# Convolved attention of a decoder on one NeuronCore: mixes of two pairs of tiles taken together, a third buffer for the turned probabilities, one buffer for the taps

## The chip, the cores and the metric

The kernel runs on one core of a Trainium2 chip. The metric is the device time of one execution in microseconds, the median of several; smaller is better. The core has TensorE (PE, with weight loads listed apart as PEld), VectorE (DVE), ScalarE (ACT), GpSimd (POOL) and SyncE (SP), which here only issues DMA. The engines run their own instruction streams in order and wait for each other through semaphores.

## The reference

A decoder of two layers on x (4 x 1024 x 256) with six stages: causal attention, attention to a context, a quantized feed-forward, the convolved attention that the change touches, attention with latents, and a feed-forward with eight experts. The touched stage, with 16 heads of 16 features:

```
def _L1_attn_ref(query, Wq, bq, Wk, bk, Wv, bv, Wo, bo, conv_w, conv_b):   # H=16, DH=16, KS=3
    Q, K, V = heads of query @ W.T + b
    scores = jnp.einsum('bhqd,bhkd->bhqk', Q, K) / np.sqrt(dh)
    x = scores.transpose(0, 2, 1, 3).reshape(b * s, h, s)
    x = lax.conv_general_dilated(x, conv_w, window_strides=(1,), padding=[(1, 1)],
                                 dimension_numbers=('NCW', 'OIW', 'NCW'))
    x = x + conv_b[None, :, None]
    weights = jax.nn.softmax(x.reshape(b, s, h, s).transpose(0, 2, 1, 3), axis=-1)
    out = jnp.einsum('bhqk,bhkd->bqhd', weights, V).reshape(b, s, e)
    return out @ Wo.T + bo
x = x + _L1_attn_ref(_layernorm(x), ...)
```

The convolution runs over key positions (three taps) and mixes heads. It is linear, so the kernel applies it to the keys: for output head h it multiplies all 256 rows of the transposed keys by per-row tap weights, at three shifts, and adds them. The scores of head h are then one product over 256 features.

## The kernel before, in words

Six stages follow each other with a barrier between. In the touched stage (`stage_conv_attention`, L1656) the 4 batches x 16 heads x 8 query tiles are 512 **units** u of 128 queries x 1024 keys; `hh = u // 8` is the head counted over all batches, `j = u % 8` the tile in it, `at = u % 128` the place in the batch. A **pair** is two units, a **group** four. All engines' streams are written out by hand as one loop over u; there is no planner.

- **Keys of a head** (`KC`, two chunks `ch` of 128 features x 1024 positions). ACT computes the outer taps k=0 and k=2 into `tap_of` (`tap`, L1993). POOL computes the middle tap (L1809), adds the two of ACT (L1813, L1817), ACT rounds the sum to fp32r (`high`, L1999, `KH`), POOL takes the rest (`low`, L1824, `KL`). This is done one to two heads ahead.
- **Scores of a unit** (`scores`, L1857): 12 matmuls of 128x128 by 128x512 (QH by KH, QH by KL, QL by KH, for two chunks and two halves) into one of three PSUM buffers of 1024 columns. `scores(u)` waits until `low_probs(u-3)` has read that buffer.
- **Softmax of a unit**: DVE `maximum` (L2116, and the bias at L2120), ACT `exps` (L2003) and `high_probs` (L2010), DVE `low_probs` (L2125): the probabilities as two f16 halves in one of four `halves`. In DVE's stream the order is maximum(u), low_probs(u-1). In ACT's it is the group's `move_mixT` where there is one, exps(u), then at most one piece of work for the keys (taps at j 1, 2, 6, 7, `high` at j 3 and 5), then high_probs(u).
- **Turning**: SP issues one DMA transpose per unit (L1791) into `probsT`, two buffers of one pair each.
- **Mix of a pair** (`mix_values`, L1871): 16 matmuls with 64-column weights (V in three bf16 parts) by 256 columns, into half of PSUM bank 6. It stands in TensorE's stream after the scores of u = 5 + 2p for pair p. After both pairs of a group ACT moves the bank (L2019, at u = 8 + 4g), TensorE transposes it back (`turn_back`, L1881, at u = 9 + 4g, ahead of the mix there) and DVE divides by the sums (L2135 to L2144, at u = 10 + 4g).
- **Fills**: the next batch's transposes, projections and the last batch's output stand after single units at fixed places of `at` (multiples of 4 from 36 to 96, and 3 to 16), 24 a batch at most.

Before the first unit, ACT and POOL build the keys of head 0 in the same way, DVE moves queries and values (L2151, L2157, L2164), and TensorE waits for the low part of both chunks (L1824).

## Time and profile before

| | us |
|---|---|
| median of 3 runs | 4256.34 (4252.75 to 4263.25) |
| profiled execution | 4279.9, span 4278.1 |
| touched stage, first to last score matmul, in that execution | 1027.45 to about 2924 |
| busy over the whole span | PE 3577.1, DVE 2966.4, ACT 2680.0, POOL 2104.9 |

The profile is one execution. Busy PE is the time in which matmuls are in flight, with modelled ends: it tells that work was there, not how fast it went. The starts of matmuls are what to measure with: the distance from one start to the next is the rate. "Idle before" names what released the engine last.

### The profile page before, as it was taken

The page shows a single profiled execution, that of the slowest core. Times are in us where ns is not written, and L with a number is a line of the kernel's source. Part 1 is how long each engine was busy: PE and PEld are TensorE (multiplying, and loading weights), DVE is VectorE, ACT ScalarE, POOL GpSimd, SP SyncE. Part 2 cuts the span into 40 slices and gives each one's busy share as a digit, 9 for nine tenths or more (in the row PEclk, how much of TensorE's full clock was granted, in tenths as well). Part 3 has the DMA queues.
Part 4 walks back from the last instruction along what each step waited for, and adds up shares of the span by engine and source line. Part 5 has one row for each costly group of instructions (what it writes and reads, how often), then busy time and mean ns, then how long its engine had stood idle before and what let it go on. Part 6 is the DMA issues. An engine that isn't in the chain of part 4 may idle for free. (4 is left out here: it accounts for less than half of the span.)

```text
span 4278.1 us, 65347 instructions
## 1 busy us (share of the span) xinstructions
PE 3577.1 (84%) x22240; PEld 2809.3 (66%) x22240; DVE 2966.4 (69%) x6077; ACT 2680.0 (63%) x3510; POOL 2104.9 (49%) x1157
## 2 busy tenths in 40 slices
PE   6877524156999999999999999996788888679999
PEld 4545311134777777777777777774567666679999
DVE  4567777875877887778877878885666666544347
ACT  3344446765877878778777878883667566333443
POOL 0044310005766667667676767770666666371004
PEclk9989756578999999999999999997899999789999
DMA  1057500005877878778877878884367477633224
GB/s 46 0 111 131 109 1 0 0 1 141 151 138 134 148 134 144 137 140 142 141 138 135 148 134 153 150 152 86 70 109 142 84 131 122 190 114 97 75 78 140
DMA packets 1571358, 470.18 MB, mean 110 GB/s; under 512 B 1507174, under 2 KB 1565159, under 8 KB 1569767
## 3 DMA queue, kind: packets, MB, share of 16 engines
q1 hardware_dynamic: 1564903, 449.40, 55.3%
q0 software_dynamic: 6144, 16.79, 1.2%
q8 instruction: 176, 2.88, 0.3%
q14 instruction: 135, 1.11, 0.1%
HBM read 49.00 MB, written 39.58 MB: 21 GB/s over the span
## 5 line engine op out<-in xcount | busy, mean ns | idle before, releaser
L2116 DVE TENSOR_REDUCE d_neg_max<-psum 128x1 f32<-128x1024 f32 x512 | 625.3, 1221 | 337.0 <-PE psum L1857 334.2
L2003 ACT ACTIVATE psum<-psum,d_bias 128x1024 f32<-128x1024 f32 x512 | 558.2, 1090 | 384.3 <-DVE d_bias L2120 383.5
L1857 PE MATMUL psum<-d_KH,d_QH 128*128 128x512 f32 x2048 | 682.7, 415 | 13.5 <-POOL d_KL L1824 7.8
L1857 PE MATMUL psum<-d_KL,d_QH 128*128 128x512 f32 x2048 | 638.1, 393 | 0.0
L1857 PE MATMUL psum<-d_KH,d_QL 128*128 128x512 f32 x2048 | 636.8, 392 | 0.0
L2125 DVE SCALAR_TENSOR_TENSOR d_halves<-psum,d_halves 128x1024 f16<-128x1024 f32 x512 | 622.6, 1216 | 14.8 <-ACT d_halves L2010 13.9
L2010 ACT ACTIVATE d_halves<-psum 128x1024 f16<-128x1024 f32 x512 | 520.6, 1017 | 3.2
L1824 POOL TENSOR_TENSOR d_KL<-d_KC,d_KH 128x1024 fp32r<-128x1024 f32 x128 | 307.3, 2401 | 338.7 <-ACT d_KH L1999 338.7
L1857 PEld LDWEIGHTS psum<-d_KH,d_QH 128*128 128x128 f32 x2048 | 362.6, 188 | 141.3 <-issue 73.3
L1857 PEld LDWEIGHTS psum<-d_KL,d_QH 128*128 128x128 f32 x2048 | 385.2, 188 | 86.9
L1857 PEld LDWEIGHTS psum<-d_KH,d_QL 128*128 128x128 f32 x2048 | 385.2, 188 | 86.7
L1809 POOL TENSOR_SCALAR d_KC<-d_K,d_taps 128x1024 f32<-128x1024 f32 x128 | 373.1, 2915 | 14.0 <-issue 14.0
L1817 POOL TENSOR_TENSOR d_KC<-d_KC,d_tap_of 128x1024 f32<-128x1024 f32 x128 | 307.1, 2399 | 138.8 <-ACT d_tap_of L1993 136.9
L2684 POOL TENSOR_TENSOR e_halves<-e_probs,e_halves 128x1102 f16<-128x1102 f32 x128 | 292.5, 2285 | 135.8 <-ACT e_halves L2785 133.8
L1813 POOL TENSOR_TENSOR d_KC<-d_KC,d_tap_of 128x1024 f32<-128x1024 f32 x128 | 308.6, 2411 | 92.1 <-ACT d_tap_of L1993 86.4
L1993 ACT ACTIVATE d_tap_of<-d_K,d_taps 128x1024 f32<-128x1024 f32 x256 | 291.5, 1140 | 0.0
L1871 PE MATMUL psum<-d_probsT,d_V 128*64 128x256 f16 x4096 | 274.1, 277 | 2.7 <-DMA d_probsT<-d_halves 2.7
L1871 PEld LDWEIGHTS psum<-d_probsT,d_V 128*64 128x64 bf16 x4096 | 204.7, 110 | 70.9 <-issue 67.4
L2778 ACT ACTIVATE e_probs<-psum,e_neg_max 128x1102 f32<-128x1102 f32 x128 | 150.7, 1177 | 112.4 <-DVE e_neg_max L2857 112.1
L3352 POOL DMA_INDIRECT f_tile<-f_expert_out,f_slots x64 | 60.6, 948 | 235.7 <-DMA f_expert_out<-f_tile 183.1
L2853 DVE TENSOR_REDUCE e_own_neg_max<-psum 128x1 f32<-128x1102 f32 x128 | 167.1, 1305 | 4.4
L3514 DVE TENSOR_TENSOR f_prod<-psum,f_silu 128x352 f32<-128x352 f32 x135 | 70.5, 522 | 143.6 <-ACT f_silu L3465 123.1
(474 smaller groups left out, 7742.6 us busy)
## 6 DMA issues: line engine op xcount, KB each, us to landing
f_weights_raw<-in_L_ffn_packed_dram SPq DMA_DIRECT2D x10, 1088.0 KB, 15.7
f_tile<-expert_rows SPq DMA_DIRECT2D x71, 128.0 KB, 2.1
f_expert_out<-f_tile SPq DMA_DIRECT2D x71, 128.0 KB, 1.7
d_probsT<-d_halves SPq DMA_TRANSPOSE x512, 4.3
f_tile<-f_kept_rows SPq DMA_DIRECT2D x64, 128.0 KB
expert_rows<-d_group_mixT SPq DMA_DIRECT2D x7, 1024.0 KB, 11.4
residual_stream<-in_x_dram SPq DMA_DIRECT2D x4, 1024.0 KB, 9.5
f_kept_rows<-residual_stream SPq DMA_DIRECT2D x4, 1024.0 KB, 8.1
```

Of the source, the lines that this page charges most:

```text
L1809: g.tensor_scalar(KC[:, ch, :], K[b % 2][:, ch, 1:S + 1], taps[:, ch, 3 * h + 1:3 * h + 2], None, ALU.mult).then_inc(tap_one.sem, 1)
L1813: g.tensor_tensor(KC[:, ch, :], KC[:, ch, :], tap_of[0][:, ch, :], ALU.add)\
L1817: g.tensor_tensor(KC[:, ch, :], KC[:, ch, :], tap_of[1][:, ch, :], ALU.add)\
L1824: g.tensor_tensor(KL[hh % 2][:, ch, :], KC[:, ch, :], KH[hh % 2][:, ch, :].bitcast(F32), ALU.subtract).then_inc(key_low.sem, 1)
L1857: last = t.matmul(scores_at(u)[:, cols], q_part[:, ch, j * P:(j + 1) * P], k_part[hh % 2][:, ch, cols], start=k == 0, stop=k == 5)
L1871: last = t.matmul(mix_bank[part * WIDE:(part + 1) * WIDE, at:at + 2 * P], V[:, k, h, :], probsT[p % 2][:, part * TB + k, :, :].rearrange(" ...
L1993: a.activation(tap_of[k // 2][:, ch, :], K[b % 2][:, ch, k:S + k], ACT.Copy, scale=taps[:, ch, 3 * h + k:3 * h + k + 1]).then_inc(tapped.s ...
L2003: a.activation(scores_at(u), scores_at(u), ACT.Exp, bias=bias[u % 2][:, 0:1])\
L2010: a.activation(halves[u % 4][:, 0, :], scores_at(u), ACT.Copy, scale=LIFT)\
L2116: v.tensor_reduce(neg_max[u % 2][:], scores_at(u), AXIS.X, ALU.max, negate=True)\
L2125: v.scalar_tensor_tensor(halves[u % 4][:, 1, :], scores_at(u), LIFT, halves[u % 4][:, 0, :], ALU.mult, ALU.subtract).then_inc(probs_low.se ...
L2684: g.tensor_tensor(halves[i % 3][:, 1, 0:W], probs[i % 3][:], halves[i % 3][:, 0, 0:W], ALU.subtract)\
```

## The change

1. TensorE takes both mixes of a group together, after the scores of u = 7 + 4g. `turn_back` stays at u = 9 + 4g, and no mix follows it there.
2. `probsT` and its semaphores `turned` get a third buffer; SP may turn pair p once pair p-3 is mixed (it was p-2).
3. `tap_of` is one buffer: ACT's tap 0 waits for the last sum of the previous head of that chunk, tap 2 for the first sum of this head (L1813). ACT's places in a head of 8 units change from taps at j 1, 2, 6, 7 to j 0, 1, 3, 6; the second `high` stays at j 5, the first goes from j 3 to j 2.
4. The keys of the very first head get their taps on DVE (2 products, 4 multiply-adds of 128x1024 f32), ahead of its moves of queries and values. ACT and POOL don't compute taps for that head.
5. POOL's middle tap becomes a product with the tap and a second product with 1.0 in one instruction.

```diff
-        tap_of = [sb(f"tap_of{i}", [P, DC, S], F32) for i in range(2)]
+        tap_of = sb("tap_of", [P, DC, S], F32)
-        probsT = [sb(f"probsT{i}", [P, 2 * TB, 2, P], F16) for i in range(2)]
+        probsT = [sb(f"probsT{i}", [P, 2 * TB, 2, P], F16) for i in range(3)]
         def both_turned(p):
-            return turned[p % 2].at(32 * (p // 2 + 1))
+            return turned[p % 3].at(32 * (p // 3 + 1))
...
-                    if i == 0 and p >= 2:
-                        sp.wait_ge(mixed.sem, mixed.at(p - 1))
+                    if i == 0 and p >= 3:
+                        sp.wait_ge(mixed.sem, mixed.at(p - 2))
...
-                        at = DC * hh + ch + 1
+                        at, seen = DC * hh + ch + 1, DC * (hh - 1) + ch + 1
                         g.wait_ge(key_low.sem, key_low.at(at - DC))
-                        g.tensor_scalar(KC[:, ch, :], K[b % 2][:, ch, 1:S + 1], taps[:, ch, 3 * h + 1:3 * h + 2], None,
-                                        ALU.mult).then_inc(tap_one.sem, 1)
+                        g.tensor_scalar(KC[:, ch, :], K[b % 2][:, ch, 1:S + 1], taps[:, ch, 3 * h + 1:3 * h + 2], 1.0,
+                                        ALU.mult, ALU.mult).then_inc(tap_one.sem, 1)
...
-                        g.tensor_tensor(KC[:, ch, :], KC[:, ch, :], tap_of[0][:, ch, :], ALU.add)\
+                        g.tensor_tensor(KC[:, ch, :], KC[:, ch, :], tap_of[:, ch, :], ALU.add)\
                             .then_inc(tap_two.sem, 1)
...
                 for hh in range(H * B):
-                    add_taps(hh)
+                    if hh:
+                        add_taps(hh)
                     low(hh)
...
-                    if u >= MIX_LAG and (u - MIX_LAG) % 2 == 0 and (u - MIX_LAG) // 2 < PAIRS * B:
-                        mix_values((u - MIX_LAG) // 2)
+                    if u >= MIX_LAG + 2 and (u - MIX_LAG - 2) % 4 == 0 and (u - MIX_LAG - 2) // 4 < GROUPS * B:
+                        mix_values((u - MIX_LAG - 2) // 2)
+                        mix_values((u - MIX_LAG - 2) // 2 + 1)
...
-                    if hh:
+                    if k == 0:
                         a.wait_ge(tap_three.sem, tap_three.at(DC * (hh - 1) + ch + 1))
+                    else:
+                        a.wait_ge(tap_two.sem, tap_two.at(DC * (hh - 1) + ch + 1))
...
-                for ch in range(DC):
-                    for k in (0, 2):
-                        tap(0, ch, k)
+                high(0, 0)
+                high(0, 1)
                 for j in range(TB):
                     queries(0, j)
-                    if j == 3:
-                        high(0, 0)
-                high(0, 1)
                 tap(1, 0, 0)
-                tap(1, 0, 2)
...
-                    if j in (1, 2) and hh + 1 < H * B:
-                        tap(hh + 1, 1, 2 * j - 2)
-                    if j in (3, 5) and hh + 1 < H * B:
-                        high(hh + 1, (j - 3) // 2)
-                    if j in (6, 7) and hh + 2 < H * B:
-                        tap(hh + 2, 0, 2 * j - 12)
+                    if j == 0 and hh + 1 < H * B:
+                        tap(hh + 1, 0, 2)
+                    if j in (1, 3) and hh + 1 < H * B:
+                        tap(hh + 1, 1, j - 1)
+                    if j in (2, 5) and hh + 1 < H * B:
+                        high(hh + 1, j // 3)
+                    if j == 6 and hh + 2 < H * B:
+                        tap(hh + 2, 0, 0)
...
+                v.wait_ge(k_ready.sem, k_ready.at(4))
+                v.wait_ge(cleared.sem, cleared.at(5))
+                for ch in range(DC):
+                    v.tensor_scalar(KC[:, ch, :], K[0][:, ch, 1:S + 1], taps[:, ch, 1:2], None, ALU.mult)\
+                        .then_inc(first_taps.sem, 1)
+                for ch in range(DC):
+                    v.wait_ge(first_taps.sem, first_taps.at(ch + 1))
+                    v.scalar_tensor_tensor(KC[:, ch, :], K[0][:, ch, 0:S], taps[:, ch, 0:1], KC[:, ch, :], ALU.mult,
+                                           ALU.add).then_inc(first_taps.sem, 1)
+                for ch in range(DC):
+                    v.wait_ge(first_taps.sem, first_taps.at(DC + ch + 1))
+                    v.scalar_tensor_tensor(KC[:, ch, :], K[0][:, ch, 2:S + 2], taps[:, ch, 2:3], KC[:, ch, :], ALU.mult,
+                                           ALU.add).then_inc(tap_three.sem, 1)
                 for k in range(4):
                     move_queries(0, k, PS[:, (4 + k) * BANK:(5 + k) * BANK])
```

## Rows read from the trace of the kernel before

**Rows 1.** Stretches: head of the stage, its 512 units (busy us and count by engine).

```profile
963.00:1027.40 64.40, 33.25 (x150) 21.76 (x148) 26.76 (x76) 26.09 (x35) 22.65 (x16) 0.80 0.51 166
1027.40:2926.00 1898.60, 1876.95 (x11096) 1460.38 (x11096) 1523.03 (x2197) 1511.81 (x1600) 1298.40 (x526) 1.00 0.80 142
```

**Rows 2.** Groups of instructions from 1060 to 2900 us (busy, mean ns, idle before).

```profile
L1857 PE MATMUL psum<-d_KH,d_QH 128*128 128x512 f32 x1984 | 661.0, 414 | 4.2 <-DVE d_halves L2125 4.2
L2116 DVE TENSOR_REDUCE d_neg_max<-psum 128x1 f32<-128x1024 f32 x496 | 605.7, 1221 | 319.3 <-PE psum L1857 316.7 <-issue 0.3
...
L1809 POOL TENSOR_SCALAR d_KC<-d_K,d_taps 128x1024 f32<-128x1024 f32 x123 | 357.5, 2907 | 0.0
...
L1817 POOL TENSOR_TENSOR d_KC<-d_KC,d_tap_of 128x1024 f32<-128x1024 f32 x124 | 297.6, 2400 | 137.3 <-ACT d_tap_of L1993 135.6
...
L1871 PE MATMUL psum<-d_probsT,d_V 128*64 128x256 f16 x3968 | 263.9, 276 | 0.0
```

**Rows 3.** Timeline of PE (start us, us, work), where it changes its kind of work.

```profile
1146.94 0.60 PE L1881 MATMUL psum<-ident,d_group_mixT 128*128 128x128 f32 x4
1147.47 1.06 PE L1871 MATMUL psum<-d_probsT,d_V 128*64 128x256 f16 x16
...
1154.18 1.06 PE L1871 MATMUL psum<-d_probsT,d_V 128*64 128x256 f16 x16
1155.17 0.73 PE L1857 MATMUL psum<-d_KH,d_QH 128*128 128x512 f32 x2
...
1158.03 0.60 PE L1911 MATMUL psum<-ident,d_ln_xn 128*128 128x128 f32 x4
1158.39 0.71 PE L1857 MATMUL psum<-d_KH,d_QH 128*128 128x512 f32 x2
```

**Rows 4.** Timeline: one unit's softmax with a tap in it, until PE goes on.

```profile
1039.65 1.22 DVE L2116 TENSOR_REDUCE d_neg_max<-psum 128x1 f32<-128x1024 f32 x1
...
1041.21 1.09 ACT L2003 ACTIVATE psum<-psum,d_bias 128x1024 f32<-128x1024 f32 x1 [0.64 <-DVE d_bias L2120]
1042.22 1.14 ACT L1993 ACTIVATE d_tap_of<-d_K,d_taps 128x1024 f32<-128x1024 f32 x1
1043.26 1.01 ACT L2010 ACTIVATE d_halves<-psum 128x1024 f16<-128x1024 f32 x1
1044.31 1.23 DVE L2125 SCALAR_TENSOR_TENSOR d_halves<-psum,d_halves 128x1024 f16<-128x1024 f32 x1 [0.56 <-ACT d_halves L2010]
1045.68 0.71 PE L1857 MATMUL psum<-d_KH,d_QH 128*128 128x512 f32 x2 [0.23 <-DVE d_halves L2125]
...
1158.23 1.22 DVE L2116 TENSOR_REDUCE d_neg_max<-psum 128x1 f32<-128x1024 f32 x1 [0.19 <-PE psum L1857]
```

**Rows 5.** Timeline of the head of the stage, up to the first score matmul.

```profile
1005.89 0.69 ACT L2033 ACTIVATE d_K<-psum,d_bk 128x512 f32<-128x512 f32 x1 [1.03 <-PE psum L1919]
...
1012.83 0.75 DVE L2151 TENSOR_SCALAR d_ln_xn<-psum,d_bq 128x512 f32<-128x512 f32 x1 [0.97 <-PE psum L1919]
1014.06 3.89 DVE L2157 TENSOR_TENSOR d_QL<-d_ln_xn,d_QH 128x256 fp32r<-128x256 f32 x8 [0.48 <-ACT d_QH L2046]
1017.87 2.73 DVE L2164 TENSOR_TENSOR d_ln_xT<-psum,d_bv 128x256 f32<-128x256 f32 x8
1022.54 4.65 POOL L1824 TENSOR_TENSOR d_KL<-d_KC,d_KH 128x1024 fp32r<-128x1024 f32 x2
1027.45 1.19 PE L1857 MATMUL psum<-d_KH,d_QH 128*128 128x512 f32 x2 [7.83 <-POOL d_KL L1824]
```

**Rows 6.** Groups of instructions of the whole span that price what is added.

```profile
L1623 DVE TENSOR_SCALAR c_gelu_again<-c_gelu_again,c_scales 128x1024 f32<-128x1024 f32 x32 | 24.0, 751 | 14.9 <-ACT c_gelu_again L1590 14.8
...
L1399 POOL COPY c_h<-c_ln_xT 128x1024 f32 x8 | 9.5, 1220 | 25.2 <-ACT c_ln_xT L230 25.2
```

**Rows 7.** A group of four units without fills (columns as in rows 1), and the transposes.

```profile
1141.15:1155.17 14.02, 14.02 (x86) 10.87 (x85) 13.10 (x21) 11.80 (x14) 11.46 (x5) 1.00 0.92 151
d_probsT<-d_halves SPq DMA_TRANSPOSE x512, 4.3
```

More of the change, by code:

```diff
@@ L1686, in stage_conv_attention @@
     tap_three = c("tap_three")
+    first_taps = c("first_taps")
     key_high = c("key_high")
@@ L1694, in stage_conv_attention @@
     probs_low = c("probs_low")
-    turned = [c(f"turned{i}") for i in range(2)]
+    turned = [c(f"turned{i}") for i in range(3)]
     mixed = c("mixed")
@@ L1865, in mix_values @@
                         t.wait_ge(v_split[2].sem, v_split[2].at(2 * p // TB // 8 + 1))
-                    t.wait_ge(turned[p % 2].sem, both_turned(p))
+                    t.wait_ge(turned[p % 3].sem, both_turned(p))
                     if p % 2 == 0 and p:
@@ L1871, in mix_values @@
                             last = t.matmul(mix_bank[part * WIDE:(part + 1) * WIDE, at:at + 2 * P], V[:, k, h, :],
-                                            probsT[p % 2][:, part * TB + k, :, :].rearrange("p i q -> p (i q)"),
+                                            probsT[p % 3][:, part * TB + k, :, :].rearrange("p i q -> p (i q)"),
                                             start=k == 0, stop=k == TB - 1)
@@ L2008, in high_probs @@
                     if u >= 4:
-                        a.wait_ge(turned[u // 2 % 2].sem, both_turned(u // 2 - 2))
+                        a.wait_ge(turned[(u // 2 - 2) % 3].sem, both_turned(u // 2 - 2))
                     a.activation(halves[u % 4][:, 0, :], scores_at(u), ACT.Copy, scale=LIFT)\
@@ L2251, in stage_conv_attention @@
         k.passed(TB * B)
-    tapped.passed(2 * DC * H * B)
-    for k in (tap_one, tap_two, tap_three, key_high, key_low):
+    first_taps.passed(2 * DC)
+    tapped.passed(2 * DC * (H * B - 1))
+    for k in (tap_one, tap_two):
+        k.passed(DC * (H * B - 1))
+    for k in (tap_three, key_high, key_low):
         k.passed(DC * H * B)
-    for k in turned:
-        k.passed(16 * U // 2 * B)
+    for i, k in enumerate(turned):
+        k.passed(32 * len(range(i, PAIRS * B, 3)))
     mixed.passed(PAIRS * B)
```

16 lines of the change are left out of this document (8 added, 8 removed).

## The prediction

> **What bounds the kernel now.** The page's chain of work that ended last lies in the expert stage and tells nothing about this one, so I read by stretches first. The 512 units take 1898.6 us, and TensorE has matmuls in flight for 1877 of them at full granted clock; DVE and ACT are busy 1523 and 1512 us, POOL 1298 [rows 1]. Then the groups' idle columns: in 1840 us the score matmuls waited 4.2 us for a PSUM buffer to be read, while the maximum on DVE waited 317 us for TensorE [rows 2]. So TensorE's stream sets the pace, the softmax follows it, and POOL and the taps are off the path. Last the timeline of PE, since "busy" does not show rate: the distance from start to start is what a change of order can gain [rows 3].
>
> From these starts: the scores of a unit take 2.86 us (1155.17 to 1158.03); a mix followed by scores 0.99 (1154.18 to 1155.17); the four transposes take 0.53 when a mix follows (1146.94 to 1147.47) but 0.36 when scores follow (1158.03 to 1158.39). A mix has 16 matmuls; one lasts 276 ns [rows 2], and all 16 last 1.06 us from first start to last end [rows 3], so the step is (1.06 - 0.28) / 15 = 0.052 us and a mix that runs on into another mix costs 16 x 0.052, some 0.85, not 0.99.
>
> **Part 1, the two mixes together.** A group without fills has four scores, transposes, mix, mix. Before: 4 x 2.86 + 0.53 + 2 x 0.99 = 13.95 us; the trace has one of 14.02 [rows 7]. After: 4 x 2.86 + 0.36 + 0.85 + 0.99 = 13.64. The gain is 0.31 us per group. The number of entries into a run of scores stays two per group, since the transposes still break them. That is the core of the argument: merging does not remove a switch from and to scores, it removes the one from transposes to mix (0.17) and a mix's tail (0.14). For 127 groups: 39 us gained. Bounds: 0 (the two mixes don't run on, and transposes before scores cost as before) to 0.53 - 0.36 + 2 x 0.14 = 0.45 per group, 57 us.
>
> What this costs: the spacing becomes less even. scores(u+3) needs low_probs(u). With the transposes alone between, the tightest unit is the first of each group: from the end of its scores to the start of the third after it lie two scores and the transposes, 2.86 + 0.36 + 2.86 = 6.08 us (before: 7.24 us at the same place and 6.71 at the tightest). The softmax with a tap in ACT's way takes 1045.68 - 1039.65 = 6.03 from the maximum to the scores it lets go [rows 4], plus 0.20 from the end of scores to the maximum (1158.03 to 1158.23) [rows 3, 4], so 6.23: 0.15 too long. Without the tap it is 1.04 shorter and hidden. Part 3 puts a tap just there, at j = 0, in one group of two: 64 x 0.15 = 10 us lost. Where DVE has norm or query work of the next batch at that place, more; I take 3 us over the stage. The other three units have 7.6 us or more.
>
> **Part 2, third buffer of probsT.** SP would wait for a mix that now comes one or two units later; with three buffers the pair needed is one older. The first half of an odd pair 2q+3 needs mix 2q, which ends 13.64 + 4 x 2.86 + 0.36 + 0.85 = 26.3 us after the group's first scores start, while the low_probs it must turn ends near 28.6 (its scores end at 22.6, the softmax takes 6). No wait, 0 us; without the buffer it would be a wait in every group. TensorE's own wait for the turned data: the second pair's last low_probs ends some 6 us after its scores and lands 4.3 us later [rows 7], 10.3; the mix comes four units after, 14.5 us. Covered by some 4 us.
>
> **Part 3, one tap buffer, other places.** Same number of instructions. ACT's first half of a head now holds three taps and a `high` where it held two and one: a group's 11.80 us [rows 7] plus 1.14 is 12.9 of 13.6, full but not over. Tap 2 now waits for POOL's first sum. Laying POOL's head out in order (2.9 + 3 x 2.4 per chunk, [rows 2], 20.2 us of 27.3 per head): the sum for chunk 1 ends about 0.9 us before ACT wants its buffer at j = 3, and that for chunk 0 about 2.0 before j = 0. If that cover went, ACT would stand with exps and high_probs queued behind the tap, and so would low_probs and scores. 0 us, as long as the middle tap does not grow; the low parts end 1.7 us ahead of the next head's scores.
>
> **Part 5, POOL's double product.** The trace has no such instruction. Below, a plain copy of the same size takes 1.22 us [rows 6]; at the same price 2.9 [rows 2]; above, a second pass would be 5.8. A faster one gains nothing, since POOL is covered. A slower one costs nothing up to some 2 us more (0.9 of cover and 1.0 that unit 3's softmax has to spare; 2.0 at j = 0). I take it as unchanged: 0 us. The row says 2.9 us for 1024 elements with one multiplication. The Trainium skill (GPSIMD Engine Reference, section 3.1, Elementwise) has a body of up to two operations bound by the port at about one cycle per element, with two no dearer than one; by that the estimate for 1024 elements is under 1 us, which this row contradicts for one operation. By either the sum stays the same.
>
> **Part 4, first head on DVE.** Keys are ready at 1006.6; the taps on DVE take 2 x 0.75 + 4 x 1.23 = 6.4 us [rows 4 to 6], up to 7.4 if the products run at the slower rate. `high` and the two low parts (4.65) then end near 1018, against 1027.2. But DVE's other work comes after: its four moves of queries (0.75 each [rows 5], 3.0, no longer paced by TensorE) end near 1016.1, where they ended at 1013.6; the low queries and values (3.89 + 2.73, from 1014.06) end at 1020.6 + 2.4 = 1023.0. TensorE waits for the values now, and the first scores start at 1023.3 instead of 1027.45. Gain 4 us (3 to 5). They start after an idle stretch either way, so the slow first matmuls (1.19 us for two, against 0.73) stay.
>
> **Sum.** -39 - 4 + 10 + 3 = -30 us against the profiled execution, 4279.9 to 4250. It stood 23.6 us above the median (0.6%), a difference that I leave in place: 4256.3 - 30 = 4226 us.
>
> **Rivals.**
>
> A. *The softmax becomes the bound in the burst.* For: ACT is at 12.9 of 13.6 us in half the groups, DVE at 13.1 in a group that has norm work [rows 7], and the tightest unit has no reserve. Against: 317 us of waiting for TensorE [rows 2]. If each group loses 0.3 us, the gain is gone but for the head: 4256 - 4 = 4252; half of that, 4237 to 4240. Chance 0.19.
>
> B. *POOL's double product is slow; the kernel is slower.* One mechanism: each us beyond 2.0 is lost twice a head (j = 0 and j = 3), 128 times. It decides at 30 / 128 = 0.25 us beyond, at 5.1 us for the instruction; at 5.8 the loss is 128 x 0.9 = 115 us against 30 gained: 4341. For: one multiplication is dearer than a sum of two inputs (2.9 against 2.4), so this instruction is already on a slow way. Against: nothing in the trace shows that a second operation doubles it. Chance 0.06.
>
> C. *Transposes' throughput.* DMA is at 0.92 of its engines in the group of 14.0 us, 151 GB/s [rows 7]. If 0.92 x 14.02 / 4 = 3.2 us per transpose is their rate, 3.4 us per unit still fits; if bursts make mixes late, the gain is lost: 4256. For it is the share of 0.92, against it 0.80 over the stage [rows 1] and 4 us of cover. The Trainium skill (DMA: Bandwidth & Descriptors, section Latency and other measured facts) puts the transpose at 261 GB/s; by that the 524 KB of a unit are an estimated 2.0 us and this rival falls. Chance 0.05.
>
> D. *The change doesn't do what it says*: two mixes side by side cost 2 x 0.99 and the transposes save only their 0.17: 127 x 0.17 = 22, with the head 4 and the losses 13: 4256 - 13 = 4243. Chance 0.08.
>
> **How the numbers follow.** The forecast (steady gain with the ring's small loss) has 0.62 and its own range of 4214 to 4238. A has 0.19, B 0.06, C 0.05, D 0.08. The range must leave no more than 0.2 out: above, it takes in D, all of A but its far end, and stops at 4252; below, the bounds of part 1 (57 gained, 5 at the head, no loss: 4194) are unlikely together, and I stop at 4206. About 0.3%, 13 us, is what a measurement of this kernel can tell: 4243.5 and 4269 are the borders. Faster: the forecast, half of A and half of D, 0.62 + 0.10 + 0.04, less some for its own upper tail, 0.74. Slower: B and a little of the rest, 0.08. Same: 0.18.
>
> **What would show it.** In PE's timeline: transposes to scores 0.36, mix to mix 0.85, mix to scores 0.99, and a group without fills of 13.7 to 13.8 us. Score matmuls' idle for d_halves from 4.2 to about 15 us, at j = 3. First scores near 1023.3, released by DVE's values. POOL's middle tap still 2.9 us. The waits of ACT for POOL (tap for the sum) near nothing; if they hold tens of us, B is at work. If score matmuls wait over 30 us for d_halves, A is; if mixes wait for probsT, C is.

## The result, and the profile after

The changed kernel takes 4217.85 us, the median of 6 runs (4215.02 to 4219.92), against 4254.45 for six runs of the kernel before (4249.5 to 4263.25). The ratio is 0.9913 with a 95% interval of 0.9903 to 0.9923: 36.6 us faster. The forecast of 4226 was 8 us too high. In the profiled executions the difference is larger, 4279.9 to 4218.73, but that is not the change: the expert stage, which nobody touched, took 592 us in the profile of before and 567 us here. It took 589 to 593 us in the four experiments beside which the kernel before had a median of 4281.98, and 560 to 569 in all others, whatever was edited. The difference between the two profiles there, 25 us, is about the 23.6 us by which the profiled execution of before stood above its median.

So the stretches of the touched stage are the thing to compare, as [rows 1] did (start and length in us, then busy us and count of PE, PEld, DVE, ACT and POOL, granted clock, DMA share and GB/s). The head, the units, and two groups without fills:

```profile
965.80:1028.80 63.00, 33.05 (x149) 21.75 (x148) 35.82 (x82) 19.13 (x29) 10.82 (x11) 0.80 0.52 170
1028.80:2885.75 1856.95, 1842.02 (x11096) 1465.03 (x11096) 1550.86 (x2197) 1520.10 (x1602) 1072.63 (x524) 1.00 0.82 145
1141.01:1154.86 13.85, 13.82 (x86) 10.86 (x86) 13.31 (x22) 11.49 (x13) 9.13 (x6) 1.00 0.86 136
1142.88:1156.72 13.84, 13.81 (x86) 10.85 (x84) 13.30 (x22) 11.51 (x12) 8.30 (x4) 1.00 0.89 147
```

The units went from 1898.6 to 1857.0 us with the same 11096 matmuls at the same full clock; a group from 14.02 [rows 7] to 13.84. The other large change is one nobody asked for: POOL is busy 226 us less.

PE's timeline from one pair of mixes to the next, to lay beside [rows 3]:

```profile
1141.01 1.94 PE L1873 MATMUL psum<-d_probsT,d_V 128*64 128x256 f16 x32
1142.88 0.74 PE L1859 MATMUL psum<-d_KH,d_QH 128*128 128x512 f32 x2
...
1145.75 0.63 PE L1859 MATMUL psum<-d_KH,d_QH 128*128 128x512 f32 x2
...
1148.51 0.60 PE L1883 MATMUL psum<-ident,d_group_mixT 128*128 128x128 f32 x4
1148.87 0.70 PE L1859 MATMUL psum<-d_KH,d_QH 128*128 128x512 f32 x2
...
1151.89 0.73 PE L1859 MATMUL psum<-d_KH,d_QH 128*128 128x512 f32 x2
...
1154.86 1.94 PE L1873 MATMUL psum<-d_probsT,d_V 128*64 128x256 f16 x32
```

Transposes to scores is 0.36 us, and the two mixes run on as 32 matmuls, 1.87 us from start to next start (predicted: 0.36, and 0.85 + 0.99 = 1.84). The units are now counted whole. I add the distances from each block's start on PE to the start of the next over all 512 units (us; a block is one unit's scores, a group's transposes, or the mixes that stand together):

| | before | after |
|---|---|---|
| scores, to whatever follows | 1498.7 | 1496.1 |
| transposes (126) to the mix, now to scores | 67.8 | 45.7 |
| mixes to what follows | 252.3 | 235.3 |
| fills | 78.0 | 78.0 |
| sum | 1896.8 | 1855.1 |

The switches gave 22.1 + 17.0 = 39.1 us; the predicted term was 39. The scores, where the waits show, were to lose 13 and gained 2.6. Broken up by place, as the excess of each distance over the tenth percentile of its kind (the same block followed by the same kind of block), summed over the stage:

| waits in front of | before | after |
|---|---|---|
| scores of j = 3 and 7 | 3.2 | 15.3 |
| mixes (after j = 3 and 7) | 0.8 | 5.3 |
| transposes (j = 1 and 5) | 32.8 | 21.0 |
| what follows the scores of j = 0 | 12.0 | 7.4 |

The two upper rows are the predicted loss, 16.6 us where 13 was said. The two lower ones, a gain of 16.4, no step of the prediction had. The rest of the 2.6 is a base distance that came out at 2.84 for 2.86.

Groups of instructions from 1060 to 2860 us, to lay beside [rows 2]:

```profile
L1859 PE MATMUL psum<-d_KH,d_QH 128*128 128x512 f32 x1984 | 660.6, 414 | 9.9 <-DVE d_halves L2127 8.9
L2118 DVE TENSOR_REDUCE d_neg_max<-psum 128x1 f32<-128x1024 f32 x496 | 605.4, 1220 | 239.6 <-PE psum L1859 234.3
L2015 ACT ACTIVATE d_halves<-psum 128x1024 f16<-128x1024 f32 x496 | 505.3, 1019 | 3.2
L1998 ACT ACTIVATE d_tap_of<-d_K,d_taps 128x1024 f32<-128x1024 f32 x247 | 283.3, 1147 | 0.0
L1810 POOL TENSOR_SCALAR d_KC<-d_K,d_taps 128x1024 f32<-128x1024 f32 x123 | 138.9, 1129 | 0.3
L1883 PE MATMUL psum<-ident,d_group_mixT 128*128 128x128 f32 x496 | 75.3, 274 | 2.0 <-ACT d_K L2043 1.1
L2146 DVE TENSOR_TENSOR d_mix<-d_group_sum,d_inv_sum 128x64 f32<-128x64 f32 x124 | 62.7, 506 | 13.6 <-DVE d_inv_sum L2143 0.9
```

Three things to read. The middle tap takes 1.13 us, not 2.9: the second operation made it faster. DVE's small product `d_mix` takes 506 ns where it took 277 (L2144 of before). And score matmuls wait 8.9 us for `d_halves` (predicted 15). The weight loads ahead of them show 26.5 us of their own, but the two don't add up to a loss: by the table above, the excess ahead of the scores of j = 3 and 7 is 15.3. One of these waits, whole:

```profile
1132.87 2.39 POOL L1825 TENSOR_TENSOR d_KL<-d_KC,d_KH 128x1024 fp32r<-128x1024 f32 x1
1133.24 2.18 DVE L2200 TENSOR_SCALAR d_ln_xn<-residual_stream,d_ln_mean_var,d_ln_rstd 128x256 f32<-128x256 f32 x1
...
1135.34 1.21 DVE L2118 TENSOR_REDUCE d_neg_max<-psum 128x1 f32<-128x1024 f32 x1
...
1136.78 1.21 DVE L2127 SCALAR_TENSOR_TENSOR d_halves<-psum,d_halves 128x1024 f16<-128x1024 f32 x1
...
1137.91 0.40 DVE L2200 TENSOR_SCALAR d_ln_xn<-residual_stream,d_ln_mean_var,d_ln_rstd 128x256 f32<-128x256 f32 x1
...
1138.05 0.74 PE L1859 MATMUL psum<-d_KH,d_QH 128*128 128x512 f32 x2 [1.47 <-DVE d_halves L2127]
```

The same normalization takes 0.40 us at 1137.91 and 2.18 at 1133.24, where it began while POOL's `low` ran and ended 0.16 us after it. The maximum behind it came late, and through the low half so did TensorE. The releaser named is `d_halves`; the cause stands three instructions ahead of it. It is so in each of the three batches, and in "all key work behind high_probs" below, where this normalization takes 0.82 us, the distance is 1.2 us shorter than in the kernel that it starts from (2.06 us).

The head of the stage, to lay beside [rows 5]:

```profile
1009.48 1.42 DVE L2206 TENSOR_SCALAR d_KC<-d_K,d_taps 128x1024 f32<-128x1024 f32 x2 [8.63 <-ACT d_K L2038]
1010.81 2.47 DVE L2210 SCALAR_TENSOR_TENSOR d_KC<-d_K,d_taps,d_KC 128x1024 f32<-128x1024 f32 x2
1013.20 2.47 DVE L2214 SCALAR_TENSOR_TENSOR d_KC<-d_K,d_taps,d_KC 128x1024 f32<-128x1024 f32 x2
...
1015.80 4.70 POOL L1825 TENSOR_TENSOR d_KL<-d_KC,d_KH 128x1024 fp32r<-128x1024 f32 x2 [20.26 <-ACT d_KH L2004]
...
1018.79 7.32 DVE L2159 TENSOR_TENSOR d_QL<-d_ln_xn,d_QH 128x256 fp32r<-128x256 f32 x8 [0.48 <-ACT d_QH L2051]
1020.60 1.42 POOL L1810 TENSOR_SCALAR d_KC<-d_K,d_taps 128x1024 f32<-128x1024 f32 x1
...
1022.11 2.38 POOL L1814 TENSOR_TENSOR d_KC<-d_KC,d_tap_of 128x1024 f32<-128x1024 f32 x1
1026.04 2.73 DVE L2166 TENSOR_TENSOR d_ln_xT<-psum,d_bv 128x256 f32<-128x256 f32 x8
...
1028.82 1.22 PE L1859 MATMUL psum<-d_KH,d_QH 128*128 128x512 f32 x2 [6.39 <-DVE d_ln_xT L2166]
```

This stage began 2.76 us later than before (its first DVE instruction at 982.45, against 979.69), so the head took 46.37 us where it took 47.76: 1.4 gained, not 4. The taps took 6.1 us from start to start of the next work (predicted 6.4) and TensorE waits for the values, as predicted. But the eight subtractions of the low queries took 7.32 us instead of the 3.89 of [rows 5]. POOL was at work beside them for the first 5.7 us. Three of the eight began inside one of its instructions and took 1.99, 1.25 and 2.56 us; the other five took 0.41 each.

### The profile page after: what moved, and what is told of

The parts are those of the page before. It is cut to its first block and busy times, and to the rows that moved or that the text cites. A ratio compares the mean times of both kernels' runs of the same rounds, so it can differ in the third digit from the quotient of the medians.

```text
span 4216.5 us, 65326 instructions
## 1 busy us (share of the span) xinstructions
PE 3539.0 (84%) x22227; PEld 2811.2 (67%) x22240; DVE 3003.9 (71%) x6083; ACT 2682.7 (64%) x3506; POOL 1868.9 (44%) x1151
## 5 line engine op out<-in xcount | busy, mean ns | idle before, releaser
L2127 DVE SCALAR_TENSOR_TENSOR d_halves<-psum,d_halves 128x1024 f16<-128x1024 f32 x512 | 622.9, 1217 | 24.6 <-ACT d_halves L2015 22.1
L1873 PE MATMUL psum<-d_probsT,d_V 128*64 128x256 f16 x4096 | 249.9, 275 | 2.3 <-DMA d_probsT<-d_halves 2.3
L1873 PEld LDWEIGHTS psum<-d_probsT,d_V 128*64 128x64 bf16 x4096 | 214.5, 110 | 49.3 <-issue 46.1
L3535 DVE TENSOR_TENSOR f_hT_low<-psum,f_hT_high 128x384 fp32r<-128x384 f32 x135 | 75.2, 557 | 116.7 <-ACT f_hT_high L3487 116.6
L3483 ACT ACTIVATE f_silu<-psum 128x352 f32<-128x352 f32 x135 | 62.8, 465 | 148.9 <-PE psum L3418 148.7
## 6 DMA issues: line engine op xcount, KB each, us to landing
expert_rows<-d_group_mixT SPq DMA_DIRECT2D x7, 1024.0 KB, 11.4
```

The costliest lines, as they stand in the source:

```text
L1873: last = t.matmul(mix_bank[part * WIDE:(part + 1) * WIDE, at:at + 2 * P], V[:, k, h, :], probsT[p % 3][:, part * TB + k, :, :].rearrange(" ...
L2127: v.scalar_tensor_tensor(halves[u % 4][:, 1, :], scores_at(u), LIFT, halves[u % 4][:, 0, :], ALU.mult, ALU.subtract).then_inc(probs_low.se ...
```

## The experiments

"Units" is the time from the first score matmul to the block behind the last scores, in the one profile of that kernel (before 1896.7, after 1855.1). How closely it repeats was not measured, but blocks that an edit leaves alone agree: the fills sum to 78.0 us in seven of the thirteen kernels, the merged mixes to 235.3 in six of ten. It contains the first unit, which took 5.0 to 5.3 us in ten kernels but 4.38 in "single product", 4.23 in "two tap buffers" and 2.87 in "reciprocals in PSUM, head". Ratios are to the kernel before, run beside each.

| kernel | median us | ratio and 95% interval | units us |
|---|---|---|---|
| mixes apart | 4249.57 | 0.9983, 0.9974 to 0.9991 | 1888.5 |
| two probsT | 4239.64 | 0.9961, 0.9948 to 0.9974 | 1871.9 |
| single product | 4254.9 | 0.9995, 0.9986 to 1.0004 | 1891.4 |
| two tap buffers, two probsT | 4235.27 | 0.9956, 0.9943 to 0.9968 | 1866.5 |
| before + merged mixes | 4262.29 | 0.9962, 0.9947 to 0.9976 | 1874.5 |
| single product, reciprocals in PSUM | 4254.14 | 0.9937, 0.9924 to 0.995 | 1868.3 |
| reciprocals in PSUM, head | 4235.37 | 0.9897, 0.9884 to 0.991 | 1851.7 |
| tap at j = 7 | 4256.64 | 0.9942, 0.993 to 0.9955 | 1866.9 |
| before + double product | 4257.99 | 1.0003, 0.9993 to 1.0014 | 1894.5 |
| j = 0 tap behind high_probs | 4216.34 | 0.9907, 0.9893 to 0.9922 | 1856.0 |
| all key work behind high_probs | 4214.35 | 0.989, 0.9873 to 0.9907 | 1858.9 |

The kernel before had medians of 4257.45 beside the first four, 4281.98 beside the next four and 4257.21 beside the last three, so only the ratios compare across these.

### Mixes apart

The changed kernel with part 1 undone, all else kept.

```diff
-                    if u >= MIX_LAG + 2 and (u - MIX_LAG - 2) % 4 == 0 and (u - MIX_LAG - 2) // 4 < GROUPS * B:
-                        mix_values((u - MIX_LAG - 2) // 2)
-                        mix_values((u - MIX_LAG - 2) // 2 + 1)
+                    if u >= MIX_LAG and (u - MIX_LAG) % 2 == 0 and (u - MIX_LAG) // 2 < PAIRS * B:
+                        mix_values((u - MIX_LAG) // 2)
```

> The changed kernel with part 1 alone undone: each pair's mix stands again after the scores of u = 5 + 2p, everything else as changed. Theory (the gain is the merging: 0.31 us per group, and the softmax gets its even spacing back): some 37 us slower than the changed kernel, near 4255, ratio to before 1.000; in PE's timeline 0.53 from transposes to mix, and the score matmuls' idle for d_halves back to about 4 us. Rival (the gain comes from the keys: POOL's faster middle tap and ACT's new places): stays at 4218 to 4225, ratio 0.992 to 0.993.

Units 1888.5: undoing it costs 33.4 us. All of the 39 us of switches comes back, and the scores' blocks fall to 1490.6 us, the lowest of all thirteen kernels. So merging is worth its structural term less some 5.5 us of waits, and the other parts together are worth 8.2 us of the units even with the mixes apart.

### Two probsT

Part 2 undone.

```diff
-        probsT = [sb(f"probsT{i}", [P, 2 * TB, 2, P], F16) for i in range(3)]
+        probsT = [sb(f"probsT{i}", [P, 2 * TB, 2, P], F16) for i in range(2)]
...
-                    if i == 0 and p >= 3:
-                        sp.wait_ge(mixed.sem, mixed.at(p - 2))
+                    if i == 0 and p >= 2:
+                        sp.wait_ge(mixed.sem, mixed.at(p - 1))
```

> The changed kernel with part 2 alone undone: two buffers of turned halves, SP waits for mix p-2 before it turns pair p. Theory of the prediction (without the third buffer there is a wait in every group): SP waits for mixes some 6 us in each of 127 groups. If that delay reached TensorE through halves or turned data, 1 us per group would give 4345. Rival (a late start of a transpose reaches nobody, since the data are needed four units later and halves come free in time): SP's waits show but the time stays 4218, within 5 us, ratio 0.990 to 0.993.

Costs 16.8 us of units. From 1060 to 2860 us:

```profile
L2015 ACT ACTIVATE d_halves<-psum 128x1024 f16<-128x1024 f32 x492 | 501.7, 1020 | 43.3 <-DMA d_probsT<-d_halves 40.9
L1859 PE MATMUL psum<-d_KH,d_QH 128*128 128x512 f32 x1965 | 655.8, 415 | 21.0 <-DVE d_halves L2127 20.2
```

The wait is not at the mix but at ACT: a transpose that starts late keeps its `halves`, and `high_probs` four units later stands for it (3.2 us in the changed kernel). The scores of j = 3 and 7 then wait 29.2 us, against 15.3.

### Single product

Part 5 undone: POOL's middle tap with one operation.

```diff
                         g.tensor_scalar(KC[:, ch, :], K[b % 2][:, ch, 1:S + 1], taps[:, ch, 3 * h + 1:3 * h + 2],
-                                        1.0, ALU.mult, ALU.mult).then_inc(tap_one.sem, 1)
+                                        None, ALU.mult).then_inc(tap_one.sem, 1)
```

> The changed kernel with part 5 alone undone: POOL's middle tap is one product again, 2.85 us instead of 1.13. Theory (POOL is covered by 0.9 us at j = 3 and 2.0 us at j = 0): no change, 4218, within 4 us; POOL's idle for tap_of falls from 547 us to about 330, ACT's taps wait for POOL in a few heads only. Rival (with one tap buffer the covers are already used by the heads that add the bias or the norm on POOL, and ACT stands): 0.5 us at both places of each head, 64 us slower, 4282.

This edit, costed at nothing, undoes the whole gain: ratio 0.9995, units +36.3 (37.2 without the first unit), while the head is 2.0 us shorter, 44.32. From 1060 to 2860 us:

```profile
L1810 POOL TENSOR_SCALAR d_KC<-d_K,d_taps 128x1024 f32<-128x1024 f32 x122 | 347.9, 2852 | 0.0
L1998 ACT ACTIVATE d_tap_of<-d_K,d_taps 128x1024 f32<-128x1024 f32 x243 | 278.5, 1146 | 0.4
L2146 DVE TENSOR_TENSOR d_mix<-d_group_sum,d_inv_sum 128x64 f32<-128x64 f32 x122 | 138.5, 1135 | 13.4 <-DVE d_inv_sum L2143 0.9
```

ACT's taps waited 0.4 us: POOL's cover held, as the prediction said. The damage came by another way. `d_mix` takes 1135 ns, and the scores of j = 5, whose buffer DVE frees behind the product at j = 2, wait: the excess ahead of them is 18.0 us (1.2 in the changed kernel) and that ahead of the transposes behind j = 5 is 19.2 (9.8). One case:

```profile
1330.15 2.37 POOL L1814 TENSOR_TENSOR d_KC<-d_KC,d_tap_of 128x1024 f32<-128x1024 f32 x1
...
1331.49 1.11 DVE L2146 TENSOR_TENSOR d_mix<-d_group_sum,d_inv_sum 128x64 f32<-128x64 f32 x1
...
1332.53 1.21 DVE L2118 TENSOR_REDUCE d_neg_max<-psum 128x1 f32<-128x1024 f32 x1
```

The product of 64 columns ends at 1332.60, within 0.1 us of POOL's sum (1332.52). With the long tap that sum lies across it; with the short one it is mostly over. Over the stage, 62 of the 128 products begin inside one of POOL's sums here and have a median of 1.95 us; in the changed kernel 35 do, in the last 0.55 us of the sum, with a median of 0.35.

### Two tap buffers and two probsT

Parts 2 and 3 undone together (the second tap buffer and the third probsT each take 8 KB of a partition, and no kernel here has both), ACT's places as before, parts 1, 4 and 5 kept.

```diff
-        tap_of = sb("tap_of", [P, DC, S], F32)
+        tap_of = [sb(f"tap_of{i}", [P, DC, S], F32) for i in range(2)]
...
-                    if j == 0 and hh + 1 < H * B:
-                        tap(hh + 1, 0, 2)
-                    if j in (1, 3) and hh + 1 < H * B:
-                        tap(hh + 1, 1, j - 1)
-                    if j in (2, 5) and hh + 1 < H * B:
-                        high(hh + 1, j // 3)
-                    if j == 6 and hh + 2 < H * B:
-                        tap(hh + 2, 0, 0)
+                    if j in (1, 2) and hh + 1 < H * B:
+                        tap(hh + 1, 1, 2 * j - 2)
+                    if j in (3, 5) and hh + 1 < H * B:
+                        high(hh + 1, (j - 3) // 2)
+                    if j in (6, 7) and hh + 2 < H * B:
+                        tap(hh + 2, 0, 2 * j - 12)
```

> The changed kernel with parts 2 and 3 undone (two tap buffers with ACT's places at j 1, 2, 3, 5, 6, 7 as before, and two buffers of turned halves, since three and two tap buffers don't fit in SBUF together); to be read beside the run with two buffers of turned halves alone. Theory of the prediction (the tap at j = 0 sits on the tightest unit): score matmuls' idle for d_halves goes down, 6 to 10 us faster than that run, near 4210. Rival (the old tap at j = 7 made ACT late for the fills, so that turn_back waited 11.5 us before and 2.0 now): those waits come back, 4218 to 4228.

Units 1866.5, 11.4 above the changed kernel and 5.4 below "two probsT". With the buffers of turned halves equal, the new places and one tap buffer cost 5.4 us, of which 1.1 is the first unit; they pay only through the third buffer that they make room for. `high_probs` waits 63.1 us for transposes here. The excess in front of the transposes is 28.5 us, against 21.0 in "two probsT", which has the new places: so most of the unforeseen gain there comes from where ACT's key work stands. It is ACT that moves the bank for these transposes. The head is 2.9 us longer here (49.31): ACT's taps come earlier, POOL works on, and five of the eight subtractions of the low queries are stretched instead of three.

### Before with merged mixes alone

The edit is the first diff of this section the other way round, on the kernel before.

> The kernel before with part 1 alone (both mixes of a group after the scores of u = 7 + 4g), two buffers of turned halves, two tap buffers, one product, first head as before. The structure of mixes and transposes gives 39 us in any case (0.31 us x 127). Theory now (the merge leaves the softmax with no reserve, so a slow middle tap on POOL and the two buffers take it back through waits of the score matmuls): some 20 to 30 us of new waits, time near 4240 to 4250, ratio 0.995 to 0.998. Rival (merging is worth its 39 us by itself): 4215 to 4225, ratio 0.991.

Ratio 0.9962, units −22.2: 39 of structure, some 17 lost.

```profile
L2011 ACT ACTIVATE d_halves<-psum 128x1024 f16<-128x1024 f32 x491 | 499.0, 1016 | 63.0 <-DMA d_probsT<-d_halves 62.0
L2145 DVE TENSOR_TENSOR d_mix<-d_group_sum,d_inv_sum 128x64 f32<-128x64 f32 x122 | 62.5, 513 | 12.7
```

Both costs of merging by itself are here: ACT waits for transposes, and `d_mix` has doubled though POOL's instructions are those of before. Merging moved it within them: in both kernels about half of the products begin inside a POOL instruction, but 45 begin here in the first 0.7 us of a tap and take 0.50 to 0.96 us, while in the kernel before most begin later in it and take 0.23. With "two tap buffers" this gives part 5 another price: from here to there it and the first head are all that differs, and the units fall by 8.0 us (0.8 of them in the first unit).

### Single product with the reciprocals in PSUM

Does the small product carry the 36 us? "Single product", and DVE writes the reciprocals into an unused column of PSUM, so that `d_mix` reads one operand there and one in SBUF. The work is the same.

```diff
-                    v.reciprocal(inv_sum[:], prob_sum[:]).then_inc(inverted.sem, 1)
+                    v.reciprocal(units[:, :, 0, WIDE - 1:WIDE], prob_sum[:]).then_inc(inverted.sem, 1)
...
-                                    inv_sum[:].to_broadcast([P, 4, HD]), ALU.mult).then_inc(normalized.sem, 1)
+                                    units[:, :, 0, WIDE - 1:WIDE].to_broadcast([P, 4, HD]), ALU.mult).then_inc(normalized.sem, 1)
```

> The changed kernel with POOL's middle tap as one product (2.85 us) as in the run that lost 37 us, and one edit more: the reciprocals of the sums are written into an unused column of the PSUM bank, so that the division's product on DVE has one input in SBUF instead of two. Theory (the loss came through that 128x64 product, 1.11 us instead of 0.50 on the mean, held until POOL's instruction is over): the product goes back to 0.23 us and 20 us or more of the loss are gone, near 4230. Rival (the loss came through ACT and the taps, the long product is a side effect): stays at 4250 to 4256.

```profile
L1810 POOL TENSOR_SCALAR d_KC<-d_K,d_taps 128x1024 f32<-128x1024 f32 x124 | 355.0, 2863 | 0.0
L2146 DVE TENSOR_TENSOR d_mix<-d_group_sum,psum 128x64 f32<-128x64 f32 x123 | 27.3, 222 | 13.5 <-DVE psum L2143 0.9
L2200 DVE TENSOR_SCALAR d_ln_xn<-residual_stream,d_ln_mean_var,d_ln_rstd 128x256 f32<-128x256 f32 x24 | 24.7, 1031 | 0.0
```

POOL's tap is as slow as in "single product", `d_mix` is down from 1135 to 222 ns, and 23.1 of the 36.3 us are back. The theory holds for these. The Trainium skill (SBUF — State Buffer, section Who interferes with whom) states that a DVE instruction with two SBUF inputs contends with a GpSimd instruction that reads SBUF. It calls the shared ports an exclusive lock, and says that the order of issue decides who blocks. The traces agree. With one operand in PSUM no product takes over 225 ns, though 123 of the 128 begin inside a POOL instruction. With both in SBUF, in the changed kernel, the 32 that begin outside take 224 to 226 ns, and of the 96 that begin inside 93 end within 0.11 us of POOL's end.

Of the other 13.2 us the traces show the place, though no edit tested the cause. DVE's other instructions on SBUF are longer here than in the changed kernel (the normalization 24.7 us against 15.6 in sum, the low queries 18.6 against 10.1), each at the same unit of all three batches: the normalizations at units 32 and 35 of a batch take 1.74 and 1.87 us instead of 0.40, the low queries at units 0 and 123 take 1.75 and 1.80 instead of 0.41. All four begin inside a sum of POOL and end 0.1 to 0.3 us behind it. And 12 of the 13.2 us are added to the distances that begin at six units of a batch (1, 33, 36, 37, 124 and 125), one or two units after these four.

### Reciprocals in PSUM, and POOL's second head behind the low queries

The changed kernel (double product) with the same edit, and POOL starting the second head only when DVE's eight subtractions at the head are done.

```diff
+                        if hh == 1:
+                            g.wait_ge(q_low.sem, q_low.at(TB))
...
+                    v.reciprocal(units[:, :, 0, WIDE - 1:WIDE], prob_sum[:]).then_inc(inverted.sem, 1)
```

> The changed kernel with the reciprocals in PSUM as above, and POOL's work for head 1 held back until DVE has finished the low parts of the queries of batch 0; the two edits are read in separate stretches. Theory: the product falls from 0.50 us to 0.23, DVE gets 34 us back, of which a part shows as fewer waits for d_halves: 5 to 12 us in the units. In the head the eight 128x256 subtractions of DVE go from 7.3 towards 5 us and the first scores come 1 us earlier. Rival: DVE has idle time where the product stands (u = 10 + 4g), so no change: within 3 us of 4218.

```profile
1011.77 4.33 DVE L2161 TENSOR_TENSOR d_QL<-d_ln_xn,d_QH 128x256 fp32r<-128x256 f32 x8 [0.48 <-ACT d_QH L2053]
...
1016.21 1.12 POOL L1810 TENSOR_SCALAR d_KC<-d_K,d_taps 128x1024 f32<-128x1024 f32 x1 [2.74 <-DVE d_QL L2161]
...
1018.81 0.73 PE L1861 MATMUL psum<-d_KH,d_QH 128*128 128x512 f32 x2 [3.40 <-DVE d_ln_xT L2168]
```

The subtractions take 4.33 us instead of 7.32, and the head 43.40 instead of 46.37 (43.26 and 43.43 in the two kernels below that share this edit): the missing part of the predicted 4 us was POOL beside DVE. The units fell by 3.4 us, but 2.4 of these are the first unit, which took 2.87 us here instead of 5.29 because TensorE's clock had not fallen; with the same edit and the same idle time it took 5.28 in both kernels below. So the short `d_mix` gains about 1 us in the changed kernel: there the 506 ns are hidden. The ratio is 0.0016 (7 us) better than the changed kernel's with overlapping intervals; 3.0 us at the head and 1 us in the units are what the traces show for it.

### A tap at j = 7 instead of j = 0

The changed kernel; ACT's tap 2 of chunk 0 one unit earlier, off the tightest unit.

```diff
-                    if j == 0 and hh + 1 < H * B:
-                        tap(hh + 1, 0, 2)
+                    if u == 0:
+                        tap(1, 0, 2)
...
-                    if j == 6 and hh + 2 < H * B:
-                        tap(hh + 2, 0, 0)
+                    if j in (6, 7) and hh + 2 < H * B:
+                        tap(hh + 2, 0, 2 * j - 12)
```

> The changed kernel with ACT's tap 2 of chunk 0 at j = 7 of the head before instead of j = 0. Theory of the prediction (the tap at j = 0 makes the tightest unit 0.15 us too long, 64 times): 8 to 12 us faster than changed, 4206 to 4210; the wait before the scores of j = 3 goes. Rival (POOL's first sum for that chunk ends about 1 us after ACT gets there at j = 7, so ACT stands and the wait moves to j = 2, or the transposes wait for ACT again): 4215 to 4225.

```profile
L1998 ACT ACTIVATE d_tap_of<-d_K,d_taps 128x1024 f32<-128x1024 f32 x247 | 282.7, 1145 | 23.8 <-POOL d_KC L1814 23.8
L1883 PE MATMUL psum<-ident,d_group_mixT 128*128 128x128 f32 x492 | 75.4, 276 | 17.0 <-ACT d_group_mixT L2024 6.8 <-ACT d_ln_xT L2031 5.5 <-ACT d_K L2043 4.2
```

The wait ahead of j = 3 fell from 10.1 to 4.2 us, so it is the tap's; but with one buffer the tap now waits for POOL's first sum with all of ACT behind it, the excess ahead of the transposes at j = 1 rose from 11.2 to 28.0, and the units lost 11.8 us. The rival won. This is the cover of part 3 (2.0 us at j = 0), used up.

### Before with the double product alone

```diff
-                        g.tensor_scalar(KC[:, ch, :], K[b % 2][:, ch, 1:S + 1], taps[:, ch, 3 * h + 1:3 * h + 2], None,
-                                        ALU.mult).then_inc(tap_one.sem, 1)
+                        g.tensor_scalar(KC[:, ch, :], K[b % 2][:, ch, 1:S + 1], taps[:, ch, 3 * h + 1:3 * h + 2], 1.0,
+                                        ALU.mult, ALU.mult).then_inc(tap_one.sem, 1)
```

> The kernel before with one edit: POOL's middle tap as a product with two operations (by the tap, by 1.0) in place of one. Theory: POOL's instruction falls from 2.85 to about 1.13 us and DVE's small product d_mix keeps its 0.23 to 0.28 us. In the kernel before the spacing of the units leaves the softmax reserve, so what DVE waits for POOL is mostly hidden: 3 to 8 us faster than before, ratio about 0.998 to 0.999. Rival: the edit is worth by itself the 36 us that it was worth in the changed kernel (ratio 0.991), and merging the mixes and this one simply add.

```profile
L1809 POOL TENSOR_SCALAR d_KC<-d_K,d_taps 128x1024 f32<-128x1024 f32 x122 | 144.2, 1182 | 0.3
L2144 DVE TENSOR_TENSOR d_mix<-d_group_sum,d_inv_sum 128x64 f32<-128x64 f32 x120 | 33.3, 277 | 12.5
```

Ratio 1.0003, units −2.2: less than the 3 to 8 us I expected, and the rival (36 us) is out. POOL's tap is 1.18 us, `d_mix` is 277 ns with either tap. In the order of before no product begins inside POOL's sums, with either tap, so there is little to be had in the units. And the head loses more than that:

```profile
1017.18 16.45 DVE L2157 TENSOR_TENSOR d_QL<-d_ln_xn,d_QH 128x256 fp32r<-128x256 f32 x8 [0.48 <-ACT d_QH L2046]
```

The eight subtractions that took 3.89 us in the kernel before [rows 5] take 16.45, six of them 2.5 us or more, because POOL, with the short tap, has its sums and `low` beside them. TensorE waits for the values behind them, and the head takes 53.64 us instead of 47.76.

### Taps behind high_probs

Both are the kernel of "reciprocals in PSUM, and POOL's second head behind the low queries" with ACT's order changed: first the tap at j = 0 alone, then all of ACT's work on keys, issued behind high_probs(u) instead of ahead of it.

```diff
                     if u < ALL:
                         high_probs(u)
+                    if j == 0 and hh + 1 < H * B:
+                        tap(hh + 1, 0, 2)
```

> e7 with one more edit: ACT's tap at j = 0 is issued behind high_probs of that unit, not ahead of it. Theory: the chain of the tightest unit is one tap (1.04 us) shorter, so the wait ahead of the scores of j = 3 (about 10 us in sum) is mostly gone: 5 to 8 us faster than e7, units near 1845 us. Rival: the tap now stands in the way of the exps of the next unit, and the wait moves to its mix or its scores (j = 4): no gain against e7, the sum of the waits as before.

> e7 with all of ACT's work on keys (taps and highs) issued behind high_probs of its unit. Theory: as e10, and the other units with a tap gain too: 8 to 12 us faster than e7, units near 1841 us. Rival: the work meets the exps of the next unit, whose bias is there by then, and POOL gets its first tap later: no gain over e10, or slower than it; scores would show waits for DVE's d_halves at j = 2, 4 and 6.

No gain in either: ratios 0.9907 and 0.989 against 0.9897, all intervals overlapping, and with the first unit's 2.4 us taken off, units 1.9 and 4.8 us longer. Ahead of j = 3 the wait fell from 10.5 to 2.0 and 2.3 us, as the theory had it. The mixes behind j = 7 and the scores of j = 7 wait longer (from 5.8 us in sum to 8.9 and 7.0), the excess ahead of the transposes of j = 5 went from 9.8 to 13.7 and 14.0, and 2.9 and 2.8 us appeared between mixes and fills. The forecast of the rival (no gain) came true, but not by its way. A tap in the way of the next exps would cost in every head. Block by block against the kernel that they start from, the distances that grew by more than 0.25 us (the first unit apart) sum to 13.3 us in the first and 19.3 in the second, and stand at eight units of a batch: 3, 5, 30, 31, 36, 37, 124, 125, and 1, 3, 5, 8, 36, 37, 124, 126. These are places behind DVE's instructions on SBUF, and those are longer. The low queries in the kernel that both start from, in the first and in the second:

```profile
L2161 DVE TENSOR_TENSOR d_QL<-d_ln_xn,d_QH 128x256 fp32r<-128x256 f32 x24 | 10.6, 441 | 0.0
L2161 DVE TENSOR_TENSOR d_QL<-d_ln_xn,d_QH 128x256 fp32r<-128x256 f32 x24 | 17.9, 745 | 0.0
L2161 DVE TENSOR_TENSOR d_QL<-d_ln_xn,d_QH 128x256 fp32r<-128x256 f32 x24 | 29.7, 1239 | 0.0
```

The one at unit 2, for example, takes 2.29 us instead of 0.43 in both: it begins inside a sum of POOL and ends 0.28 us behind it. Later taps on ACT moved POOL's sums onto DVE's work. No edit separated this from the rival's way, but the places speak for it.

## Why the prediction was right, and where it was not

**Part 1 (39 us gained).** Right in kind and size: 0.36, 1.87 for 1.84, 39.1 us in sum. TensorE's stream was the bound and is still.

**Its cost (10 + 3).** Right in mechanism: the scores of j = 3, released by DVE's `d_halves`, through the tap at j = 0 ("tap at j = 7" shows it) and DVE's norm work (the wait at 1138.05; long not by its own work but by POOL beside it). The size was 16.6 with the mixes counted. What the term left out is a gain of about the same size, 16.4: transposes and what follows j = 0 wait less. For the transposes, "two tap buffers" puts most of it (28.5 against 21.0) on the places of ACT's key work; for the rest it was not separated. In place of the net loss of 13 the runs show a gain of 2.6: luck, since no step of mine had it.

**Part 2 (0, and a wait in every group without it).** Right: 16.8 us without it. The prediction looked for that wait at SP; its price was paid two steps on, at ACT, for `halves`.

**Part 3 (0).** The cover held (ACT waited 0.0 us for POOL), and using it up costs 11.8 us. Taken alone against the old places it costs 5.4, or 4.3 without the first unit.

**Part 5 (0: "a faster one gains nothing, since POOL is covered").** This is the step that failed, and the good sum hides it by luck. Its duration was outside the bounds I took: 1.13 us, just under the 1.22 of a copy [rows 6], the end I did not choose. The page cited in the prediction (the Trainium skill, GPSIMD Engine Reference, section 3.1, Elementwise) has less than 1 us by estimate; that is near the two-operation form, and far from the 2.85 of the one-operation form. And its worth is 36.3 us in the changed kernel, since with the merged mixes and the new places the long tap puts POOL's sums across a DVE product with two SBUF inputs (23.1 us of it shown by the reciprocals in PSUM) and, it seems, across DVE's norm and query work. "Covered" was answered for the semaphores alone; an engine can be held up by another one on which it never waits. The term of zero came out because the rest of the sum was made from rows of the kernel before, where `d_mix` was hardly disturbed (277 ns, and 225 alone): with the single product, which I thought equal, the kernel takes 4254.9 us, the "same" of my chances. So the forecast was right for a kernel with a short tap, and I forecast a long one.

**Part 4 (4 us gained).** Order of events right, 1.4 measured. The step that failed is the low queries at 3.89: 7.32 beside POOL. This too goes back to the tap: with the one operation that I had reckoned with ("single product") they take 5.16 and the head 44.32, 3.4 gained; the short tap takes 2.0 of it back. With POOL held back the whole head gains 4.4.

**Rivals.** A did not happen (8.9 us of waits for `d_halves` against the 30 that I had set as its sign), though it is what "single product" looks like (22.8 and 51.6 at the weight loads). B was wrong in sign: the instruction got faster. C: mixes waited 5.1 us in all for transposes, before 5.9. D is refuted by the 1.87.

Of the price of the parts, each undone alone: merging 33.4, third buffer 16.8, double product 36.3 us. They add to 86.5, over twice the 41.6 that the units gained. So the parts don't add. The double product gives the units 2.2 us in the kernel before (and costs its head 5.9), 8.0 together with the new first head in the kernel with merged mixes and the old tap places, and 36.3 with the new ones.

## What to carry to other kernels

Ask of an engine off the critical path not only who waits for it, but beside what it runs: a POOL instruction can stretch a short DVE one on SBUF to POOL's own end, and a reordering on TensorE or ACT, or a faster instruction on POOL itself, can bring the two together. Compare the mean of such small instructions before and after; a doubled mean (277 to 513 ns) of an unchanged instruction is the sign, and for this product one operand in PSUM was the cure. Undo each part by itself before believing a sum that comes out right.

## What the runs showed of the hardware

- POOL's product of 128 x 1024 f32 with a per-partition scalar takes 2.85 to 2.92 us with one operation and 1.13 to 1.20 us with two (the second by 1.0), in four kernels of the one and nine of the other.
- DVE's product of 128 x 64 with two SBUF inputs has means of 277, 506 and 1135 ns by what POOL does beside it; with one operand in PSUM it has 221 or 222 in four kernels, whatever POOL does. With two SBUF inputs it takes 224 to 228 ns in all nine kernels when no POOL instruction is running as it begins. If it begins inside POOL's sum or two-operation product, it ends 0.07 to 0.1 us behind it, with hardly an exception. If it begins early in the one-operation product, it ends 1.65 us before that product's recorded end (48 products of "single product", 45 of "before + merged mixes"): the 2.85 us instruction holds DVE no longer than the 1.13 us one.
- DVE's subtraction of 128 x 256 with two SBUF inputs takes 0.41 us alone and up to 2.58 us when it begins inside a POOL instruction.
- TensorE's clock after a short idle is not a matter of the idle time alone. Stretches from the first score matmul on, of "reciprocals in PSUM, and POOL's second head" and of "j = 0 tap behind high_probs", both after 3.4 us without a matmul:

```profile
1018.81:1022.40 3.59, 3.59 (x16) 2.96 (x17) 0.52 (x1) 2.32 (x2) 0.96 (x1) 1.00 0.00 0
```

```profile
1020.23:1023.80 3.57, 3.57 (x8) 2.81 (x9) 0.00 (x0) 2.31 (x2) 0.96 (x1) 0.50 0.00 0
```

  The granted clock is 1.00 (2.4 GHz) in one and 0.50 (1.2 GHz) in the other, 16 matmuls against 8 in the same time. After 6.4 us of idle, in the changed kernel, it was 0.50. Such a start is worth 2.4 us and is no merit of an edit.
